# A two-layer kernel on one core: block inverses of a head gathered into one step of its loop, gram products one step further ahead

## The chip, the cores and the metric

The kernel runs on one NeuronCore of a Trainium2 chip. Its engines are TensorE (PE), VectorE (DVE), ScalarE (ACT), GpSimd (POOL) and SyncE (SP), which here only issues transfers. Each takes its instructions in the order in which they are written, and engines wait for one another by semaphores. The metric is the device time of one execution in microseconds, lower is better. The kernel before was timed three times: 1269.07, 1272.46 and 1273.2 us, median 1272.46 us.

## The reference

The input is `x` of 4 batches, 256 rows and 256 columns. Two layers follow one another, each an attention block and a feed-forward block behind a modulated layer norm. The change lies in the attention block of the first layer, a gated delta rule over 16 key heads with two value heads each:

```python
qkvz = hidden_states @ W_qkvz                 # per key head: q, k (128 each), v, z (256 each)
conv = silu(sum(xp[:, j:j + Tv, :] * conv_w[:, j] for j in range(4)))   # over q, k, v
beta = jax.nn.sigmoid(b)
alpha = jnp.exp(-jnp.exp(A_log) * jax.nn.softplus(a + dt_bias))
q = _l2norm(q) * DK ** (-0.5)
k = _l2norm(k)
def step(S, inp):                             # one row of the sequence after the other
    q_t, k_t, v_t, a_t, b_t = inp
    S = S * a_t[..., None, None]
    err = jnp.einsum('bhkv,bhk->bhv', S, k_t)
    v_new = (v_t - err) * b_t[..., None]
    S = S + k_t[..., None] * v_new[..., None, :]
    o = jnp.einsum('bhkv,bhk->bhv', S, q_t)
    return (S, o)
og = o * _silu(z)
og = og * jax.lax.rsqrt(jnp.mean(og * og, axis=-1, keepdims=True) + EPS) * norm_weight
return og.reshape(Bv, Tv, VDIM) @ W_out
```

The kernel computes the recurrence in blocks of 128 rows. For each value head and each half of the sequence, the rows of `v_new` are the solution of a triangular system of size 128.

## The kernel before, in words

The first layer runs as a loop of 64 steps: key head `kh` from 0 to 15 outside, batch `b` from 0 to 3 inside. A step of each engine is written in `pe_step`, `act_step`, `dve_step`, `pool_step`. In step (kh, b) several stages lie side by side, for different batches. `beside` picks the batch that is so many steps ahead.

- **q and k, 8 steps ahead** (`LEAD_QK`): `pe_qk` multiplies, `act_tap0` and `dve_tap` do the convolution in place, and `act_silu_qk` ends it.
- **Gram products, 7 steps ahead** (`LEAD_GRAM`): `pe_gram0` and `pe_gram1` form k·k and q·k. DVE scales them (`dve_scales`, `dve_scan`, `dve_bp`) into the block tiles `BP`, of which there are eight, two key heads by four batches.
- **v and z, 3 steps ahead** (`LEAD_VZ`), in the same manner, with a transpose of v (`pe_vt`) one step later.
- **The solve of this step**: `pe_solve` multiplies with the inverse of the triangular blocks in `UT` and with `BP`. `act_y` and `dve_r2` carry the pieces between its three parts. `pe_o` gives the output, `dve_og` gates it.
- **The output of the step before**: `act_ss` sums the squares (line 693), `pool_ro` takes the power -0.5 on GpSimd (line 998), `act_ogn` scales (line 701), `pe_ot` transposes (line 444), `act_ots` evicts (line 724), `pe_f` multiplies with the output weights (line 454), and `dve_acc` adds.

The inverses take a way of their own. The 32-row diagonal blocks of the next key head go from `BP` to a scratch tensor in HBM (`sp_blocks_in`, line 1076) and back into `Dm`, where each of 64 partitions holds one block (`sp_blocks_turn`, line 1085). GpSimd inverts all 64 at once by elimination (`pool_inverse`): for j from 0 to 30 one product (line 1023) and one subtraction (line 1026), each waiting for the one before. Those 31 pairs are dealt out over the four steps of a key head by `SPLIT`: 7, 12, 7 and 5 pairs, and `pool_ro` of the same step stands behind them in GpSimd's order. ACT writes the transpose `Tt` in two halves, in steps 2 and 3 (`act_turn`, line 718). Both results go out to HBM (`sp_blocks_out`, line 1097) and come back, spread over partitions, into `U` and `UT` (`sp_blocks_read`, lines 1107 and 1112). There `pe_merge` builds the inverses of size 64 and 128 out of those of size 32, in four phases. Each is a run of small matmuls into one PSUM bank (bank 7), with an eviction by ACT behind it (`act_merge`): the product of the diagonal (lines 391 and 392), the 32-row parts (394 to 396), the lower 64-row part (398), the upper one (400). Step 0 merges batches 0 and 1, step 1 merges batches 2 and 3. Steps 2 and 3 have no merges.

All transfers are issued by SP in one order that is written out by hand in its block: for each key head the turn, the reads, the loads of weights and of `alb`, the blocks of three batches, the out-transfer, the reads of the first two batches. A transfer whose condition isn't met holds up those written behind it.

## Time and profile before

| | |
|---|---|
| median of three timed runs | 1272.46 us |
| lowest, highest | 1269.07, 1273.2 us |
| span of the profiled execution | 1270.6 us |
| PE busy | 1168.6 us (92%) |
| VectorE busy | 914.6 us (72%) |
| ScalarE busy | 831.6 us (65%) |
| GpSimd busy | 751.5 us (59%) |
| GpSimd on the elimination, lines 1023 and 1026 | 551.8 us |

The page gives a span for the profiled execution, from its first to its last instruction, and no time beside it. The span lies within the three timed runs. The busy time of an engine is the time in which one of its instructions ran. For PE it hides that matmuls follow one another in a pipe. Busy time is an average over the whole program. The loop of the first layer takes up the stretch from about 105 to 1075 us, and only that stretch is touched.

### The profile page before, as it was taken

How to read it: one execution, taken by the hardware profiler on the slowest of the kernel's cores; microseconds unless marked ns; L12 is line 12 of the kernel's file. 1: busy time of each engine (PE TensorE's matmuls, PEld its weight loads, DVE VectorE, ACT ScalarE, POOL GpSimd, SP SyncE). 2: the span in 40 equal slices, each digit the busy share in tenths (PEclk: the TensorE clock that was granted, in tenths of full speed). 3: DMA queues.
4: the chain of work that ended last, by engine and by line, in shares of the span. 5: the costliest groups of instructions: out<-in, count | busy, mean ns of one | idle time of the engine just before them, and what ended most of it. 6: DMA issues, size and time to landing. Idle time of an engine off the chain costs nothing. (4 is left out here: it accounts for less than half of the span.)

```text
span 1270.6 us, 30469 instructions
## 1 busy us (share of the span) xinstructions
PE 1168.6 (92%) x10744; PEld 1002.5 (79%) x10744; DVE 914.6 (72%) x2304; ACT 831.6 (65%) x2289; POOL 751.5 (59%) x1187
## 2 busy tenths in 40 slices
PE   7787998999999999999999999999998688998986
PEld 6687887888888888888888888888887577776754
DVE  6786787788879797878888888879793414337764
ACT  6334776777777676777777777777675556218973
POOL 3275758586867777776858586858676601104211
PEclk9776999999999999999999999999998979999988
DMA  5212134314040313121222314040214130002000
GB/s 177 64 55 51 66 73 44 83 34 111 7 112 19 99 31 87 37 80 40 80 45 73 65 52 111 6 113 14 62 29 129 25 108 1 1 1 72 2 10 25
DMA packets 143430, 72.82 MB, mean 57 GB/s; under 512 B 116744, under 2 KB 132624, under 8 KB 141360
## 3 DMA queue, kind: packets, MB, share of 16 engines
q1 hardware_dynamic: 143280, 70.89, 22.5%
q8 instruction: 86, 1.41, 0.5%
q14 instruction: 64, 0.52, 0.1%
HBM read 57.06 MB, written 13.78 MB: 56 GB/s over the span
## 5 line engine op out<-in xcount | busy, mean ns | idle before, releaser
L1023 POOL TENSOR_TENSOR tmp<-Dm,Tn 64x31 f32<-64x31 f32 (+15 forms) x496 | 260.5, 525 | 104.0 <-DMA Dm<-blk_in_scratch 69.9
L1026 POOL TENSOR_TENSOR Tn<-Tn,tmp 64x31 f32<-64x31 f32 (+15 forms) x496 | 291.3, 587 | 38.8
L832 DVE SCALAR_TENSOR_TENSOR cv<-bank,cw,cv 128x255 f32<-128x255 f32 (+2 forms) x384 | 155.2, 473 | 145.0 <-ACT cv L631 144.8
L832 DVE SCALAR_TENSOR_TENSOR cqk<-bank,cw,cqk 128x255 f32<-128x255 f32 (+2 forms) x384 | 155.0, 472 | 16.5 <-ACT cqk L631 16.4
L998 POOL TENSOR_TENSOR ro<-ss,mhalf 128x4 f32<-128x4 f32 x64 | 68.0, 1062 | 158.2 <-issue 97.7
L892 DVE SCALAR_TENSOR_TENSOR BP<-bank,cj,E 128x512 f32<-128x512 f32 (+1 forms) x256 | 140.4, 611 | 2.6 <-DVE cj L877 0.3
L454 PE MATMUL bank<-wo,OTs 128*128 128x256 f32 x512 | 132.1, 392 | 0.9 <-ACT OTs L724 0.9
L693 ACT ACTIVATE junk<-og 128x129 f32<-128x129 f32 x256 | 79.6, 311 | 51.6 <-issue 39.4
L701 ACT ACTIVATE ogn<-og,ro 128x128 f32<-128x128 f32 x256 | 81.9, 393 | 44.4 <-POOL ro L998 44.1
L433 PE MATMUL bank<-Y,BP 128*128 128x128 f32 x512 | 95.7, 290 | 7.4 <-ACT Y L664 6.1
L454 PEld LDWEIGHTS bank<-wo,OTs 128*128 128x128 f32 x512 | 91.3, 193 | 12.0 <-ACT OTs L724 1.0
L338 PE MATMUL bank<-hh,wvz_hi 128*128 128x256 f32 x256 | 84.2, 329 | 9.0 <-ACT hT L645 9.0
L433 PEld LDWEIGHTS bank<-Y,BP 128*128 128x128 f32 x512 | 73.0, 193 | 19.4 <-ACT Y L664 19.4
L348 PE MATMUL bank<-wvz_hi,hh 128*128 128x256 f32 x256 | 83.7, 327 | 0.9
L308 PE MATMUL bank<-hh,wqk_hi 128*128 128x256 f32 x256 | 80.4, 314 | 3.1 <-DVE cqk L832 3.1
L664 ACT ACTIVATE Y<-bank 128x256 f32<-128x256 f32 x128 | 48.9, 382 | 51.6 <-PE bank L420 50.5
L318 PE MATMUL bank<-sqk 128*128 128x512 f32 x128 | 67.9, 613 | 8.8 <-DVE BP L892 8.8
L308 PE MATMUL bank<-hh,wqk_lo 128*128 128x256 f32 x256 | 74.8, 292 | 0.0
L308 PE MATMUL bank<-hl,wqk_hi 128*128 128x256 f32 x256 | 74.6, 292 | 0.0
L338 PE MATMUL bank<-hh,wvz_lo 128*128 128x256 f32 x256 | 74.2, 290 | 0.0
L338 PE MATMUL bank<-hl,wvz_hi 128*128 128x256 f32 x256 | 74.0, 289 | 0.0
L348 PE MATMUL bank<-wvz_hi,hl 128*128 128x256 f32 x256 | 73.2, 286 | 0.0
(210 smaller groups left out, 3326.9 us busy)
## 6 DMA issues: line engine op xcount, KB each, us to landing
rvz<-in_L_attn_W_qkvz SPq DMA_DIRECT2D x16, 512.0 KB, 5.5
x<-alpha_scratch SPq DMA_DIRECT2D x8, 1024.0 KB, 6.6
alb<-alpha_scratch SPq DMA_DIRECT2D x7, 1024.0 KB, 6.3
rqk<-in_L_attn_W_qkvz SPq DMA_DIRECT2D x16, 256.0 KB, 2.6
wo<-in_L_attn_W_out SPq DMA_DIRECT2D x16, 256.0 KB, 6.2
blk_in_scratch<-BP SPq DMA_DIRECT2D x256, 16.0 KB, 1.5
tinv_scratch<-Tn SPq DMA_DIRECT2D x32, 128.0 KB, 2.2
tinv_t_scratch<-Tt SPq DMA_DIRECT2D x32, 128.0 KB, 2.2
```

What stands on the lines that cost most here:

```text
L308: last = nc.tensor.matmul(bQK[:, t * T:(t + 1) * T], wqk[p][w][:, k, t * DK:(t + 1) * DK], h[:, k, b * T:(b + 1) * T], start=(k + n == 0), ...
L338: last = nc.tensor.matmul(bV[:, t * T:(t + 1) * T], wvz[p][w][:, k, t * DK:(t + 1) * DK], h[:, k, b * T:(b + 1) * T], start=(k + n == 0), ...
L348: last = nc.tensor.matmul(bZ[:, c * 256:(c + 1) * 256], h[:, k, b * T + c * P:b * T + (c + 1) * P], wvz[p][w][:, k, R * DK:2 * R * DK], st ...
L433: last = nc.tensor.matmul(o, block_of(p, b, h, 0, 0, c), Y[:, 0, h, :], start=True, stop=(c == 0))
L454: last = nc.tensor.matmul(bF[:, c * D:(c + 1) * D], OTs[:, h, c, :], wo[p][:, h, :], start=(h == 0), stop=(h == R - 1))
L693: nc.scalar.activation(junk[:], og[b % 2][:, c, h, :], ACT.Square, accum_out=ss[b % 2][:, n:n + 1]).then_inc(sem("ss"), 1)
L701: nc.scalar.activation(ogn[:, c, h, :], og[b % 2][:, c, h, 0:DK], ACT.Copy, scale=ro[b % 2][:, n:n + 1]).then_inc(sem("ogn"), 1)
L832: nc.vector.scalar_tensor_tensor(d, bk[:, t * T:(t + 1) * T - s], cw[p][:, first + t, TAPS - 1 - s:TAPS - s], d, ALU.mult, ALU.add).then_i ...
L892: nc.vector.scalar_tensor_tensor(dst, g, cj[i][:, c, h:h + 1], e, ALU.mult, ALU.mult).then_inc(sem("bp"), 1)
L998: nc.gpsimd.tensor_tensor(ro[b % 2][:], ss[b % 2][:], mhalf[:, 0:4], ALU.pow).then_inc(sem("ro"), 1)
L1023: pool_step_done(nc.gpsimd.tensor_tensor(t, Dm[:, j, j + 1:BLK].unsqueeze(2).broadcast_to([SLOTS, r, c]), Tn[:, j, 0:c].unsqueeze(1).broad ...
L1026: pool_step_done(nc.gpsimd.tensor_tensor(Tn[:, j + 1:BLK, 0:c], Tn[:, j + 1:BLK, 0:c], t, ALU.subtract), kh * NTS + 2 * j + 4)
```

## The change

The gram products, and with them the block tiles, move one step further ahead, from 7 to 8 steps, and q and k from 8 to 9. The block tiles become a ring of nine (`bp_of`) instead of two sets of four. All four batches of a key head merge in step 0 (`merges`), so that steps 1 to 3 have no merges. The phases now take all batches at once for the 32-row parts. The 64-row parts run as lower of batches 0 and 1, then lower of 2 and 3 alternating with upper of 0 and 1, then upper of 2 and 3. GpSimd's elimination is dealt out over steps 0 to 2, as 16, 5 and 10 pairs, and the blank start of the next one moves from step 0 to step 3. The four blocks' return into `Dm` is now a single transfer of 256 KB behind the reads, where it was two groups of four. The reads of `U` and `UT` take all four batches at once, in 3 and 4 transfers of twice the size. Both weight splits move to step 0. Some small tiles share memory with others to make room.

The core of the diff:

```diff
             E2 = sb("E2", [P, R, P], ctx=s1)
 
-            BP = [BP0, sb("BP1", [P, B, 6 * R, P], ctx=s1)]
-            Dm = sb("Dm", [SLOTS, BLK, BLK], ctx=s1)
+            BP1 = sb("BP1", [P, RING - B, 6 * R, P], ctx=s1)
+
+            def bp_of(kh, b):
+
+                n = (kh * B + b + RING - 1) % RING
+                return BP0[:, n] if n < B else BP1[:, n - B]
+
...
-            LEAD_QK, LEAD_GRAM, LEAD_VZ = 2 * B, 2 * B - 1, 3
+            LEAD_QK, LEAD_GRAM, LEAD_VZ = 2 * B + 1, 2 * B, 3
...
+            def pe_merge_64(kh, low, high):
+
+                wait(nc.tensor, "u_evac", kh * U_EV + (3 if high is None else 5 if high == 0 else 7))
+                lows = slots(range(2 * low, 2 * low + 2)) if low is not None else ()
+                highs = slots(range(2 * high, 2 * high + 2)) if high is not None else ()
+                for n in range(2 * NC * R):
+                    if lows:
+                        last = merge_low(kh, *lows[n])
+                    if highs:
+                        last = merge_high(kh, *highs[n])
                 last.then_inc(sem("u_mm"), 1)
...
             def merges(b):
-                return b < 2
+                return b == 0
...
                     if last:
                         pe_ot(*last, 2 * (now + 2))
-                    pe_merge(kh, p, b, 1)
                     if vz:
                         pe_v(*vz, 1, (1,))
+                    pe_merge_32(kh)
                     if last:
                         pe_f(*last, 0)
-                    pe_merge(kh, p, b, 2)
-                    if last:
                         pe_f(*last, 1)
-                    pe_merge(kh, p, b, 3)
+                    pe_merge_64(kh, 0, None)
                     if vz:
                         pe_z(*vz, 0)
-                    pe_solve(kh, p, b, 0)
+                    pe_merge_64(kh, 1, 0)
                     if vz:
                         pe_z(*vz, 1)
+                    pe_solve(kh, p, b, 0)
+                    pe_merge_64(kh, None, 1)
                     pe_solve(kh, p, b, 1)
                     if vt:
...
                 if merges(b):
                     if last:
                         act_ogn(*last)
-                    act_merge(kh, p, b, 0)
+                    act_merge_diag(kh)
                     act_before_ots(kh, b)
                     if last:
                         act_ots(*last)
-                    act_merge(kh, p, b, 1)
                     if vz:
                         act_tap0(*vz, "v", bV, cv, 2)
+                    act_merge_32(kh)
                     if qk:
                         act_tap0(*qk, "qk", bQK, cqk, 0)
-                    act_merge(kh, p, b, 2)
-                    act_merge(kh, p, b, 3)
+                    act_merge_low(kh, 0)
                     if vz:
                         act_silu_v(*vz)
+                    act_merge_high(kh, 0)
+                    act_merge_low(kh, 1)
                     act_y(kh, p, b, 0)
-                    splits(kh, p, b, act_split_qk, act_split_vz)
                     if qk:
                         act_silu_qk(*qk)
+                    act_merge_high(kh, 1)
                     if vz:
                         act_silu_z(*vz)
                     act_y(kh, p, b, 1)
                     if vt:
                         act_vs(*vt)
+                    splits(kh, p, b, act_split_qk, act_split_vz)
                 else:
                     act_y(kh, p, b, 0)
...
+                if kh and exists(kh + 1, 0, 0):
+                    split_vz(kh + 1, 1 - p)
+                if exists(kh + 3, 0, 0):
                     split_qk(kh + 3, 1 - p)
-                if b == 0 and kh and exists(kh + 1, 0, 0):
-                    split_vz(kh + 1, 1 - p)
...
                     dve_acc(*last)
                 if merges(b):
-                    dve_r2(kh, p, b)
-                    splits(kh, p, b, dve_split_qk, dve_split_vz)
                     ahead = beside(kh, p, b, LEAD_GRAM + 1)
                     if ahead:
                         scans(ahead, 0, R)
-                    dve_og(kh, p, b)
+                    dve_r2(kh, p, b)
                     if ahead:
                         scans(ahead, R, 2 * R)
+                    dve_og(kh, p, b)
+                    splits(kh, p, b, dve_split_qk, dve_split_vz)
 
...
-            SPLIT = ((0, 7), (7, 19), (19, 26), (26, BLK - 1))
-            LAST_SPLIT = ((0, 6), (6, 14), (14, 21), (21, BLK - 1))
+            SPLIT = ((0, 16), (16, 21), (21, BLK - 1))
...
             def pool_step(kh, p, b):
-                if kh + 1 < NKH:
-                    if b == 0:
-                        pool_vpow(kh + 1, 1 - p)
-                        pool_inverse_start(kh + 1)
-                    pool_inverse(kh + 1, *(SPLIT if kh + 2 < NKH else LAST_SPLIT)[b])
+                if b < len(SPLIT) and kh + 1 < NKH:
+                    pool_inverse(kh + 1, *SPLIT[b])
+                if b == B - 1 and kh + 2 < NKH:
+                    pool_inverse_start(kh + 2)
                 pool_ro(kh, p, b)
+                if b == 0 and kh + 1 < NKH:
+                    pool_vpow(kh + 1, 1 - p)
 
...
-            def sp_blocks_turn(kh, lo, hi):
-                for b in range(lo, hi):
+                                      bp_of(kh, b)[r, 0:4 * R:2, r]).then_inc(sem(f"blk_dr{b}"), 16)
+
+            def sp_blocks_turn(kh):
+                for b in range(B):
                     wait(nc.sync, f"blk_dr{b}", (kh + 1) * 16 * NBLK)
                 wait(nc.sync, "t_step", kh * NTS)
-                for n in range(NBLK):
-                    s = slice((n * B + lo) * PER_B, (n * B + hi) * PER_B)
-                    nc.sync.dma_start(Dm[s].rearrange("s j i -> s (j i)"),
-                                      blkin_dr[n, lo:hi].rearrange("b c h j i -> (b c h) (j i)")).then_inc(sem("blk_in"), 16)
...
+            def sp_blocks_read(kh):
+                wait(nc.sync, "y", at(kh, 0, 2))
                 wait(nc.sync, "t_out0", (kh + 1) * 32)
                 for n in range(NBLK - 1):
...
                 wait(nc.sync, "t_out1", (kh + 1) * 32)
                 for n in range(NBLK):
...
-                    sp_blocks_in(kh + 1, B - 1)
-                    sp_blocks_turn(kh + 1, B - 1, B)
-                    sp_blocks_read(kh, 1)
+                    ahead = kh + 2 < NKH
+                    if ahead:
+                        sp_blocks_in(kh + 2, 0)
                     if kh + 3 < NKH:
-                        sp_load_qk(kh + 3)
                         sp_load_alb(kh + 3)
-                    if kh + 2 < NKH:
+                    if ahead:
                         sp_load_vz(kh + 2)
...
-                    if kh + 2 < NKH:
-                        for b in range(B - 1):
-                            sp_blocks_in(kh + 2, b)
+                    if ahead:
+                        sp_blocks_in(kh + 2, 1)
+                        sp_blocks_in(kh + 2, 2)
+                    if kh + 4 < NKH:
+                        sp_load_qk(kh + 4)
                     sp_blocks_out(kh + 1)
-                    sp_blocks_read(kh + 1, 0)
-                sp_blocks_read(NKH - 1, 1)
+                    if ahead:
+                        sp_blocks_in(kh + 2, B - 1)
+                    sp_blocks_read(kh + 1)
+                    if ahead:
```

The other hunks write the phases of `pe_merge` and `act_merge` as functions of their own (`pe_merge_diag`, `pe_merge_32`, `merge_low` and `merge_high` with the same matmuls; `act_merge_diag` and `act_merge_32` with evictions of twice the width; `act_merge_low` and `act_merge_high` with the same as before). They also double the tile `nrm`, move one qk product, one gram product and one weight split from the loop into the code ahead of it, and place small tiles.

GpSimd around the start of a key head, where `ro` is the power of a step's output, `vsc` that of the scales, and `tmp<-Dm,Tn` and `Tn<-Tn,tmp` are one pair of the elimination. Before:

```order
L1023 TENSOR_TENSOR tmp<-Dm,Tn 64x31
L1026 TENSOR_TENSOR Tn<-Tn,tmp 64x31
L998 TENSOR_TENSOR ro<-ss,mhalf 128x4
L993 TENSOR_TENSOR vsc<-nrm,npow 128x16
L1012 MEMSET Tn 64x1024
L1013 AFFINE_SELECT Tn<-Tn 64x1024
L1023 TENSOR_TENSOR tmp<-Dm,Tn 64x31
L1026 TENSOR_TENSOR Tn<-Tn,tmp 64x31
```

In the changed kernel, where `DT` holds `Dm` and `Tt`:

```order
L1048 TENSOR_TENSOR Tn<-Tn,tmp 64x31
L1021 TENSOR_TENSOR ro<-ss,mhalf 128x4
L1034 MEMSET Tn 64x1024
L1035 AFFINE_SELECT Tn<-Tn 64x1024
L1021 TENSOR_TENSOR ro<-ss,mhalf 128x4
L1045 TENSOR_TENSOR tmp<-DT,Tn 64x31
L1048 TENSOR_TENSOR Tn<-Tn,tmp 64x31
```

and behind the first 16 pairs of the same key head:

```order
L1045 TENSOR_TENSOR tmp<-DT,Tn 64x256
L1048 TENSOR_TENSOR Tn<-Tn,tmp 64x16x16
L1021 TENSOR_TENSOR ro<-ss,mhalf 128x4
L1016 TENSOR_TENSOR vsc<-nrm,npow 128x16
L1045 TENSOR_TENSOR tmp<-DT,Tn 64x255
L1048 TENSOR_TENSOR Tn<-Tn,tmp 64x15x17
```

The blank start now stands ahead of the last `ro` of the key head before. Between that `ro` and the next one stand 16 pairs, where there were 7 with `vsc` and the blank start ahead of them.

SP from the out-transfers of one key head to the blocks of the next. Before:

```order
L1097 DMA tinv_scratch<-Tn 32x1024 x2
L1097 DMA tinv_t_scratch<-Tt 32x1024 x2
L1107 DMA U<-tinv_scratch 32x8x32 x3
L1112 DMA UT<-tinv_t_scratch 32x8x32 x4
L1085 DMA Dm<-blk_in_scratch 12x1024 x4
L1076 DMA blk_in_scratch<-BP 32x4x32 x4
L1085 DMA Dm<-blk_in_scratch 4x1024 x4
L1107 DMA U<-tinv_scratch 32x8x32 x3
L1112 DMA UT<-tinv_t_scratch 32x8x32 x4
```

In the changed kernel:

```order
L1114 DMA tinv_scratch<-Tn 32x1024 x2
L1114 DMA tinv_t_scratch<-DT 32x1024 x2
L1097 DMA blk_in_scratch<-BP 32x4x32 x4
L1122 DMA U<-tinv_scratch 32x16x32 x3
L1127 DMA UT<-tinv_t_scratch 32x16x32 x4
L1104 DMA DT<-blk_in_scratch 64x1024
L1097 DMA blk_in_scratch<-BP 32x4x32 x4
L1075 DMA x<-alpha_scratch 128x2048
```

The return into `Dm` stood ahead of the second reads, in two parts with the blocks of the fourth batch between them. Now it is one transfer, and all reads stand ahead of it.

PE at the 64-row parts of step 0. `U,BP` is the lower part, `UT,A2` the upper one. Before:

```order
L338 MATMUL bank3<-hl,wvz_hi1 128x256
L454 MATMUL bank5<-wo0,OTs 128x256 x2
L398 MATMUL bank7<-U,BP1 64x64 x8
L454 MATMUL bank5<-wo0,OTs 128x256 x2
L400 MATMUL bank7<-UT,A2 64x64 x8
L348 MATMUL bank3<-wvz_hi1,hh 128x256
```

In the changed kernel:

```order
L476 MATMUL bank5<-wo0,OTs 128x256 x4
L407 MATMUL bank7<-U,BP0 64x64 x8
L354 MATMUL bank3<-wvz_hi1,hh 128x256
L354 MATMUL bank3<-wvz_lo1,hh 128x256
L354 MATMUL bank3<-wvz_hi1,hl 128x256
L354 MATMUL bank3<-wvz_hi1,hh 128x256
L354 MATMUL bank3<-wvz_lo1,hh 128x256
L354 MATMUL bank3<-wvz_hi1,hl 128x256
L407 MATMUL bank7<-U,BP1 64x64
L411 MATMUL bank7<-UT,A2 64x64
L407 MATMUL bank7<-U,BP1 64x64
L411 MATMUL bank7<-UT,A2 64x64
```

The lower part of the second two batches now alternates, matmul by matmul, with the upper part of the first two. The output product `wo0,OTs` stands ahead of the first lower part as a whole.

## Rows read from the trace of the kernel before

**Rows 1.** Loop: stretch, us, busy PE, PEld, DVE, ACT, POOL (count), clock, DMA share, GB/s.
```profile
140.00:1050.00 910.00, 864.99 (x8550) 755.53 (x8550) 700.70 (x1588) 644.94 (x1721) 639.33 (x1008) 0.98 0.26 62
```

**Rows 2.** PE's timeline, first matmul of a step: start us, us, engine line operation.
```profile
235.91 0.59 PE L318 MATMUL bank<-sqk 128*128 128x512 f32 x1
...
593.38 1.02 PE L318 MATMUL bank<-sqk 128*128 128x512 f32 x2
...
610.59 0.59 PE L318 MATMUL bank<-sqk 128*128 128x512 f32 x1
...
627.43 0.59 PE L318 MATMUL bank<-sqk 128*128 128x512 f32 x1
...
640.13 0.59 PE L318 MATMUL bank<-sqk 128*128 128x512 f32 x1
...
652.51 0.59 PE L318 MATMUL bank<-sqk 128*128 128x512 f32 x1
...
950.56 0.59 PE L318 MATMUL bank<-sqk 128*128 128x512 f32 x1
```

**Rows 3.** PE's timeline in step 0 of a key head, phases of the merge.
```profile
597.81 0.21 PE L391 MATMUL bank<-U,BP 32*32 32x32 f32 x1
597.82 0.21 PE L392 MATMUL bank<-U,BP 32*32 32x32 f32 x1
...
598.31 0.19 PE L392 MATMUL bank<-U,BP 32*32 32x32 f32 x1
...
601.47 1.14 PE L398 MATMUL bank<-U,BP 64*64 64x64 f32 x16
```

**Rows 4.** GpSimd's timeline, same key head; brackets: idle time before, what ended it.
```profile
595.90 2.89 POOL L993 TENSOR_TENSOR vsc<-nrm,npow 128x16 f32<-128x16 f32 x1 [0.43 <-DVE nrm L872]
...
604.35 0.23 POOL L1023 TENSOR_TENSOR tmp<-Dm,Tn 64x31 f32<-64x31 f32 x1 [3.25 <-DMA Dm<-blk_in_scratch]
...
608.02 1.97 POOL L1026 TENSOR_TENSOR Tn<-Tn,tmp 64x135 f32<-64x135 f32 x1
...
613.26 1.05 POOL L998 TENSOR_TENSOR ro<-ss,mhalf 128x4 f32<-128x4 f32 x1 [0.75 <-POOL Tn L1026]
...
627.42 0.89 POOL L1023 TENSOR_TENSOR tmp<-Dm,Tn 64x255 f32<-64x255 f32 x1
```

**Rows 5.** VectorE's timeline, the two weight splits of that key head.
```profile
607.92 1.22 DVE L855 TENSOR_TENSOR wvz_lo<-rvz,wvz_hi 128x1024 fp32r<-128x1024 f32 x1
...
625.12 0.68 DVE L851 TENSOR_TENSOR wqk_lo<-rqk,wqk_hi 128x512 fp32r<-128x512 f32 x1
```

**Rows 6.** ScalarE and PE in step 2: scaled output and its transpose.
```profile
633.06 1.28 ACT L701 ACTIVATE ogn<-og,ro 128x128 f32<-128x128 f32 x4
...
634.39 0.33 PE L444 MATMUL bank<-eye,ogn 128*128 128x128 f32 x1 [0.42 <-ACT ogn L701]
```

**Rows 7.** Step 3: ScalarE's turn, SP's issues, and from the page a landing time.
```profile
648.44 1.11 ACT L718 ACTIVATE Tt<-Tn 64x512 f32<-64x512 f32 x1
...
645.22 1.73 SPq L1076 DMA_DIRECT2D blk_in_scratch<-BP  x4
...
649.57 0.78 SPq L1097 DMA_DIRECT2D tinv_t_scratch<-Tt  x2
650.88 1.33 SPq L1107 DMA_DIRECT2D U<-tinv_scratch  x3
652.26 1.93 SPq L1112 DMA_DIRECT2D UT<-tinv_t_scratch  x4
...
rqk<-in_L_attn_W_qkvz SPq DMA_DIRECT2D x16, 256.0 KB, 2.6
```

**Rows 8.** PE's idle spells in two steps, and a row of the busy table.
```profile
206.62 0.71 PE L420 MATMUL bank<-R,UT 128*128 128x128 f32 x4 [2.77 <-issue]
...
971.25 1.11 PE L444 MATMUL bank<-eye,ogn 128*128 128x128 f32 x4 [2.95 <-ACT ogn L701]
...
973.00:975.00 2.00, 2.00 (x27) 1.76 (x22) 0.00 (x0) 1.59 (x6) 1.76 (x4) 0.50 0.92 334
```

More of the change, by code:

```diff
@@ L798, in act_step @@
                         act_vs(*vt)
-                    if b == B - 1:
+                    if not merges(last[2]):
                         act_ogn(*last)
@@ L802, in act_step @@
                         act_tap0(*qk, "qk", bQK, cqk, 0)
-                    if b < B - 1:
+                    if merges(last[2]):
                         act_ogn(*last)
@@ L809, in act_step @@
                     act_ots(*last)
[L810 removed]
+                    if kh + 1 < NKH and b >= 2:
                         act_turn(kh + 1, b - 2)
```

204 lines of the change are left out of this document (99 added, 105 removed).

## The prediction

> **What bounds the kernel now.** The busy times come first: over the loop PE is busy 865 of 910 us, and no other engine above 701 [rows 1]. Next comes PE's own timeline, to get the length of each step. One key head takes 17.2, 16.8, 12.7 and 12.4 us for its four steps, 59.1 us from 593.38 to 652.51 [rows 2]. The twelve key heads from 235.91 to 950.56 average 59.55 us [rows 2]. The first two steps are longer because they hold the merges. PE's idle time is 45 of 910 us, 2.9 per key head [rows 1]. One piece of it is a wait for the scaled output ahead of its transpose, 0.42 us here [rows 6]. So PE sets the pace, and the reader should see that the other engines wait for it.
>
> GpSimd comes closest to it, not by busy share but as a chain. It waits 3.25 us for `Dm`, starts its pairs at 604.35, 11.0 us into the key head [rows 4], and has to end them before ScalarE turns the second half at 648.44, 8.3 us into step 3 [rows 7]. Between them it has to give `ro`, without which the output of a step isn't scaled. That chain is what the change rearranges.
>
> **What the change does on PE.** No matmul goes away. Per key head two gathered steps become one. The first phase of a merge takes 0.53 us for two batches (597.81 to the last start 598.31 and its spacing), and so does the second roughly. A 64-row part takes 1.07 us for two batches, 16 passes from 601.47 with the next product behind them [rows 3]. Step 0 now has these once more: 0.53 + 0.53 for the 32-row phases and, if lower and upper parts run at the same time, one more 1.07. With 0.2 for one more change of shape, the new step 0 is 17.2 + 2.3 = 19.5 us. Step 1 becomes like step 2. PE alone would need 19.5 + 12.7 + 12.4 + 12.4 = 57.0 us, 2.1 less than the 59.1.
>
> Would the alternating halves overlap? Lines 391 and 392, which read different rows of the array and write different partitions of one bank, start 0.01 us apart, a pair every 0.03 us [rows 3]. I take full overlap. Without it the step costs 1.07 more. The Trainium skill, "TensorEngine Tiling (Array Packing)", Restrictions and Gotchas, says that different row tiles cannot access the same PSUM bank at once. By that rule the halves in bank 7 would run one after the other. The trace speaks against it for the 32-row pairs.
>
> The wider evictions, 256 to 512 columns, cost ScalarE no more in all, since there are half as many. They lie under v, the transposes and both output products. Weight splits at the end of step 0 and the earlier scans hide in VectorE's idle time, which grows in step 0. The gram product one step earlier costs nothing in the loop.
>
> **What it does to GpSimd's chain.** Two things move. The reads are now all issued ahead of the return into `Dm`, and 16 pairs stand ahead of the first `ro`. I follow them from step 3, times counted from that step's start (640.13 in the trace):
> - the turn of the second half ends at 9.4, and `Tt` goes out from 9.4 to 10.2 [rows 7];
> - blocks of the fourth batch 1.7, reads of `U` 1.3, reads of `UT` 1.9 [rows 7], with gaps of 0.1 each: the return is issued at 15.6. The reads are twice as large, but SP's issue time goes by count, and the count is the same;
> - a transfer of 256 KB lands 2.6 us after issue [rows 7]: `Dm` is there at 18.2, which is 5.8 us into the next step 0. That is 5.2 earlier than now.
>
> From there (counted from step 0), 16 pairs. In the trace they take from 604.35 to 627.42 less 1.8 for the `ro` between them, 21.3 us [rows 4]. That figure contains the slowing by both weight splits: the subtraction at 608.02 took 1.97 us under the split at 607.92 [rows 4, 5]. In the new order both splits again fall into the 16 pairs, so I keep 21.3. It could be 2 less if they missed each other, and hardly more. The Trainium skill, "SBUF — State Buffer", Who interferes with whom, says a VectorE instruction with two SBUF inputs blocks one of GpSimd that reads SBUF. The trace agrees.
>
> So the pairs end at 27.1, `ro` takes 1.05 [rows 4] to 28.2, and the scaling 1.28 [rows 6] to 29.5. The transposes start at 29.6. Without waiting they would stand at 19.5 + 6.5 = 26.0, since in step 2 they stand 6.96 after the step's start with 0.42 idle [rows 2, 6]. **PE waits 3.6 us** in step 1 of each key head. Queued behind the transposes on PE are the third solve, the output, its product and z, and on ScalarE behind the scaling the first tap of v. From transposes to the end of the step are 5.7 us [rows 2, 6], so step 2 starts at 35.3. The other two steps end at 60.3 us.
>
> The remaining pairs fit this length. After `ro` come the scale power, 2.89 [rows 4], 5 pairs (6.7 at the mean of the sixteen, 21.3 / 16) and `ro`, ending 28.2 + 10.7 = 38.9, 3.6 into step 2. Then come 10 pairs, at most 13.3 at that mean and less since their sizes fall, and `ro`, ending at most 5.6 into step 3. The scaling asks for them about 4 into each step (it ran at 633.06, 5.6 into step 2, behind a tap that now follows it [rows 6]). I add nothing, and keep 0.5 each for the range.
>
> **The clock.** After idle spells of 2.77 and 2.95 us PE ran slow: at 971.25 four transposes took 1.11 us, and the table has a granted clock of 0.50 at 973 [rows 8]. That is 1.2 instead of 2.4 GHz. A wait of 3.6 us in every key head should bring it down most times. The two microseconds of that row, with PE busy throughout, lose 1 us of work, and the slow stretch began before them and at 971.25 at the latest, so the spell there cost 2 or more. I take 2 per key head, between 1 and 3. So a key head takes 62.3 us, 2.75 above 59.55.
>
> **The sum.** Key heads 1 to 13 give 13 × 2.75 = +36. Key head 0 gets the same wait early, about +4. Key head 1 has a stall of 2.77 with its slow clock behind it [rows 8] that the new wait may cover, −3. In key head 14 PE waits for `ogn` already [rows 8] and the elimination bounds; it starts 5.2 earlier now. Key head 15 saves the 2.1 of the merges. Together I estimate −7. That makes +30. The profiled span is 1270.6 and the median 1272.5, so the forecast is about 1302; I say 1300 us.
>
> **The rivals.**
> - **A, GpSimd late but the clock stays.** A key head takes 60.3, 0.75 more: 13 × 0.75 − 6 = +4, 1277 us (1268 to 1284). For it: waits like the 0.42 us of rows 6 occur in every key head with the mean clock at 0.98 [rows 1]. Against it: both spells near 3 us brought it down.
> - **B, GpSimd in time, so PE bounds: faster.** A key head takes about 57.3: 13 × −2.25 and −8 at the ends, −37, 1235 us (1228 to 1246). It decides where the first `ro` is done by 24.6 us after the start of step 0, 3.6 us sooner than I have it. The whole chain, 31 pairs and three powers, would have to shrink too. For it: `Dm` lands after one transfer, and its landing and the pairs' slowing are the two terms I estimate. Against it: both together give perhaps 2.5.
> - **C, in between.** Pairs and landing 1.5 to 2.5 us faster, PE waiting 1 to 2 us with the clock up: a key head of 58.5, 13 × −1.05 − 6 = −20, 1252 us (1246 to 1267).
> - **D, the change's alternation doesn't do what it says.** The halves don't overlap, step 0 is 20.6, the wait in step 1 shrinks by the same 1.1 and the key head stays at 60.3. It then favours A's number, since the wait falls to 2.5. The rule of the Trainium skill on banks, quoted above, would make this the case.
>
> **How the numbers follow.** The forecast gets 0.46, A with D 0.23, C 0.17, B 0.14. The forecast's own range is 1284 to 1316 from the clock's 1 to 3 us and half a microsecond either way in `Dm`. The range 1246 to 1316 leaves out most of B and a little above. A measurement of this kernel tells about 0.3%, 3.8 us, from no change. Faster than 1268.7: B, C and a little of A, 0.32. Within: the middle of A, 0.12. Slower: 0.56.
>
> **What would show it.** Right: PE's `ot` transposes of step 1 wait for `ogn`, and that for `ro`, which follows GpSimd's sixteenth pair without a gap; idle 3 to 4 us before them once per key head; `Dm` landing 5 to 6.5 us into step 0; granted clock of 0.5 in short stretches over the whole loop; step 0 of 19 to 20 us, steps 2 and 3 at 12.4 to 13. Wrong: GpSimd waits for the sums of squares ahead of the first `ro`, or step 1 is under 14 us, or the clock stays at 1.0. If step 0 is over 21, an eviction or the read of `UT` is late, which I held for covered (the read lands about 5 us into the step, and the second phase stands at 7).

## The result, and the profile after

The changed kernel takes 1311.6 us (median, 1305.4 to 1315.3) and the kernel before 1270.8 beside it on the same chip: 1.031 times as long, 95% interval 1.027 to 1.035. Forecast were 1300 us, in a range of 1246 to 1316, and a slower kernel. The profiled execution has a span of 1313.6 us, 43.0 over the 1270.6 of before. Ratios and intervals here and below leave out three executions that lay far above the rest: one of 1326 us of the kernel before, one of 2700 and one of 4572 us of two later kernels.

The first look goes to the busy table, cut at PE's step starts. One key head of the changed kernel, and then a stretch of its second step and the whole loop (stretch, its length, busy time of PE, PEld, DVE, ACT, POOL, granted clock, DMA share, GB/s):

```profile
565.55:584.47 18.92, 18.82 (x315) 16.56 (x313) 12.82 (x29) 13.29 (x31) 10.92 (x22) 1.00 0.40 101
584.47:604.33 19.86, 14.79 (x91) 13.64 (x89) 13.18 (x29) 10.95 (x34) 18.25 (x23) 0.83 0.17 44
604.33:616.70 12.37, 12.28 (x90) 11.00 (x89) 11.26 (x28) 9.26 (x23) 10.40 (x22) 1.00 0.13 29
616.70:629.08 12.38, 12.29 (x90) 11.01 (x89) 11.06 (x29) 9.87 (x27) 3.43 (x3) 1.00 0.21 47
...
595.00:602.00 7.00, 5.93 (x24) 5.65 (x25) 3.30 (x8) 5.13 (x15) 6.53 (x8) 0.51 0.00 0
...
140.00:1080.00 940.00, 845.70 (x8470) 758.25 (x8468) 690.35 (x1576) 634.08 (x1647) 640.10 (x1020) 0.95 0.25 57
```

Before, the loop had PE busy 865 of 910 us at a clock of 0.98 [rows 1]. Now it is busy 846 of 940 at 0.95. In this key head steps 0, 2 and 3 have PE busy without a gap. All the idle time is in step 1, which holds no merge: 14.8 of 19.9 us busy, and the clock at half speed for part of it. Over eleven key heads the four steps average 19.4, 19.2, 12.4 and 12.4 us, 63.3 in all. Before they were 17.2, 17.1, 12.9 and 12.4, 59.55 [rows 2]. Step 0 is 18.9 us where nothing disturbs it. Its average is higher because three of the eleven waited 0.2 to 1.4 us ahead of 32-row products, for which the trace names no cause, and because the clock fell behind the longest of these waits: that step 0 took 22.0 us.

PE's timeline at the first merge phase shows where the 43 us are (start, duration, then the operation, idle time before it in brackets). The third row is the stall of one step 1:

```profile
123.98 0.18 PE L390 MATMUL bank<-U,BP 32*32 32x32 f32 x1 [1.64 <-DMA U<-tinv_scratch]
...
254.84 0.21 PE L390 MATMUL bank<-U,BP 32*32 32x32 f32 x1
...
596.07 1.11 PE L466 MATMUL bank<-eye,ogn 128*128 128x128 f32 x4 [5.07 <-ACT ogn L722]
...
1011.86 0.23 PE L390 MATMUL bank<-U,BP 32*32 32x32 f32 x1 [1.76 <-issue]
...
1069.52 0.18 PE L390 MATMUL bank<-U,BP 32*32 32x32 f32 x1 [0.16 <-issue]
```

The L390 rows are key heads 0, 2, 14 and 15. The same phases of the kernel before started at 113.79, 240.34, 953.55 and 1014.90. So the way to the first merge grew by 10.2 us (I put this down to the longer lead; no run tries it alone), key heads 0 and 1 by 4.3, the twelve key heads 2 to 13 by 43.8 (3.65 each). Key head 14 shrank by 3.7, and what comes after key head 15's merge by 11.6. The sum is +43.0.

GpSimd, ScalarE and SyncE at the same place tell what PE waited for. GpSimd's timeline:

```profile
566.41 1.01 POOL L1021 TENSOR_TENSOR ro<-ss,mhalf 128x4 f32<-128x4 f32 x1 [1.23 <-issue]
572.96 0.23 POOL L1045 TENSOR_TENSOR tmp<-DT,Tn 64x31 f32<-64x31 f32 x1 [5.54 <-DMA DT<-blk_in_scratch]
...
593.70 1.01 POOL L1021 TENSOR_TENSOR ro<-ss,mhalf 128x4 f32<-128x4 f32 x1
...
616.05 0.24 POOL L1048 TENSOR_TENSOR Tn<-Tn,tmp 64x31 f32<-64x31 f32 x1
...
626.66 0.94 POOL L1034 MEMSET Tn<- 64x1024 f32 x1 [7.86 <-ACT DT L739]
```

ScalarE's timeline, the scaling in step 1 and the turn in step 3:

```profile
594.74 1.28 ACT L722 ACTIVATE ogn<-og,ro 128x128 f32<-128x128 f32 x4 [4.74 <-POOL ro L1021]
...
561.61 1.10 ACT L739 ACTIVATE DT<-Tn 64x512 f32<-64x512 f32 x1
```

SyncE's issues in step 3 and the step after it, and from the page the landing time of the return, in us:

```profile
562.74 1.01 SPq L1114 DMA_DIRECT2D tinv_t_scratch<-DT  x2
563.84 1.81 SPq L1097 DMA_DIRECT2D blk_in_scratch<-BP  x4
565.75 1.44 SPq L1122 DMA_DIRECT2D U<-tinv_scratch  x3
567.23 2.08 SPq L1127 DMA_DIRECT2D UT<-tinv_t_scratch  x4
569.48 0.45 SPq L1104 DMA_DIRECT2D DT<-blk_in_scratch  x1
...
DT<-blk_in_scratch SPq DMA_DIRECT2D x16, 256.0 KB, 3.5
```

Read them as a chain. The turn ends 9.6 us into step 3, the return is issued at 16.3, and `Dm` is there at 572.96, 7.4 into step 0. Sixteen pairs take 20.7 us with nothing between them, `ro` follows without a gap, then the scaling, then PE after 5.07 us of idle time. The last pair ends at 616.29, 0.4 before step 3. ScalarE turns this result only in the middle of step 3: the turn starts at 625.15, 8.9 us behind the last pair. GpSimd has one more `ro` to do in that time and then stands idle for 7.9 us, until the turn is over. That delay is the key to the experiments.

### The profile page after: what moved, and what is told of

It is laid out like the page before. It is cut to its first block and busy times, and to the rows that moved or that the text cites. A ratio compares the mean times of both kernels' runs of the same rounds, so it can differ in the third digit from the quotient of the medians.

```text
span 1313.6 us, 30101 instructions
## 1 busy us (share of the span) xinstructions
PE 1157.3 (88%) x10744; PEld 1011.2 (77%) x10744; DVE 911.0 (69%) x2304; ACT 827.4 (63%) x2225; POOL 742.6 (57%) x1187
## 5 line engine op out<-in xcount | busy, mean ns | idle before, releaser
L1045 POOL TENSOR_TENSOR tmp<-DT,Tn 64x31 f32<-64x31 f32 (+15 forms) x496 | 256.1, 516 | 134.7 <-DMA DT<-blk_in_scratch 99.4
L1048 POOL TENSOR_TENSOR Tn<-Tn,tmp 64x31 f32<-64x31 f32 (+15 forms) x496 | 286.0, 577 | 38.9
L466 PE MATMUL bank<-eye,ogn 128*128 128x128 f32 x256 | 46.2, 310 | 78.7 <-ACT ogn L722 78.5
L476 PEld LDWEIGHTS bank<-wo,OTs 128*128 128x128 f32 x512 | 98.1, 202 | 14.2 <-issue 1.8
L455 PE MATMUL bank<-Y,BP 128*128 128x128 f32 x512 | 102.8, 315 | 1.5 <-ACT Y L686 0.2
L466 PEld LDWEIGHTS bank<-eye,ogn 128*128 128x128 f32 x256 | 32.9, 157 | 83.0 <-ACT ogn L722 82.8
L455 PEld LDWEIGHTS bank<-Y,BP 128*128 128x128 f32 x512 | 83.2, 220 | 10.9 <-ACT Y L686 10.9
L927 DVE SCALAR_TENSOR_TENSOR og<-bank,vsc,hT 128x256 f32<-128x256 f32 x128 | 55.9, 479 | 49.3 <-PE bank L457 49.3
L344 PE MATMUL bank<-hh,wvz_hi 128*128 128x256 f32 x256 | 80.7, 315 | 4.1 <-ACT hT L667 4.1
L1034 POOL MEMSET Tn<- 64x1024 f32 x16 | 15.1, 944 | 114.7 <-ACT DT L739 114.7
```

The costliest lines, as they stand in the source:

```text
L344: last = nc.tensor.matmul(bV[:, t * T:(t + 1) * T], wvz[p][w][:, k, t * DK:(t + 1) * DK], h[:, k, b * T:(b + 1) * T], start=(k + n == 0), ...
L455: last = nc.tensor.matmul(o, block_of(kh, b, h, 0, 0, c), Y[:, 0, h, :], start=True, stop=(c == 0))
L466: last = nc.tensor.transpose(bOT[:, n * P:(n + 1) * P], ogn[:, c, h, :], ident)
L476: last = nc.tensor.matmul(bF[:, c * D:(c + 1) * D], OTs[:, h, c, :], wo[p][:, h, :], start=(h == 0), stop=(h == R - 1))
L1045: pool_step_done(nc.gpsimd.tensor_tensor(t, Dm[:, j, j + 1:BLK].unsqueeze(2).broadcast_to([SLOTS, r, c]), Tn[:, j, 0:c].unsqueeze(1).broad ...
L1048: pool_step_done(nc.gpsimd.tensor_tensor(Tn[:, j + 1:BLK, 0:c], Tn[:, j + 1:BLK, 0:c], t, ALU.subtract), kh * NTS + 2 * j + 4)
```

## The experiments

Theory: PE's wait in step 1 is one chain through GpSimd, and only the chain's placement is at fault. Rival: the merged step itself is dearer on PE, and the wait for `ro` is its shadow.

**The turn at the front of step 3** (in `act_step`).

```diff
                 else:
+                    if kh + 1 < NKH and b == B - 1:
+                        act_turn(kh + 1, 1)
                     act_y(kh, p, b, 0)
...
-                    if kh + 1 < NKH and b >= 2:
-                        act_turn(kh + 1, b - 2)
+                    if kh + 1 < NKH and b == 2:
+                        act_turn(kh + 1, 0)
```

> Edit: ScalarE turns the second half of the inverses at the front of step 3 instead of behind its output eviction; all else as in the changed kernel. Theory (one chain through GpSimd): in the changed kernel the turn stands 9.6 us into step 3, the return into Dm is issued at 16.3 and lands at 19.8, 7.4 into step 0; 16 pairs, ro and the scaling follow and PE waits 5.1 us. The elimination is over 0.4 us before step 3 starts, so the turn can be 8 us sooner. The reads then wait for the last Y of step 3 (7.8 into the step), so the return gains 4.7 us of the 8. PE's wait goes from 5.1 to about 0.4 us, the clock stays up, a key head goes from 62.4 to about 57: 1240 us (1228 to 1262). Rival 1 (the pace is set by PE's merged step and its clock, the wait for ro is a shadow of it): the wait moves to another semaphore and the time stays within 5 us of 1311. Rival 2 (the landing of Dm is slowed by the transfers queued ahead of it, not by its issue): Dm gains under 2 us, 1285 us.

Measured 1234.2 us (0.972 of before, 0.968 to 0.977), and in a second run 1236.3 (0.971, 0.968 to 0.974). One instruction a key head, moved, gives back 77 us. GpSimd's timeline, the busy table of steps 3, 0 and 1, and ScalarE's turn:

```profile
533.61 0.23 POOL L1047 TENSOR_TENSOR tmp<-DT,Tn 64x31 f32<-64x31 f32 x1 [1.67 <-DMA DT<-blk_in_scratch]
...
554.33 1.01 POOL L1023 TENSOR_TENSOR ro<-ss,mhalf 128x4 f32<-128x4 f32 x1
```

```profile
517.30:530.00 12.70, 12.27 (x90) 10.99 (x89) 11.25 (x29) 9.88 (x27) 5.10 (x8) 1.00 0.38 74
530.00:549.00 19.00, 18.90 (x315) 16.63 (x314) 13.31 (x29) 13.38 (x31) 14.37 (x28) 1.00 0.27 82
549.00:562.40 13.40, 12.17 (x90) 11.04 (x89) 12.72 (x28) 10.92 (x34) 12.54 (x14) 1.00 0.25 65
```

```profile
519.53 1.11 ACT L739 ACTIVATE DT<-Tn 64x512 f32<-64x512 f32 x1 [0.98 <-POOL Tn L1050]
```

Both rivals are out: the time left 1311 far behind, and `Dm` gained 3.8 us. `Dm` now lands 3.6 us into step 0 (7.4 without the edit), the first `ro` starts at 24.3 (28.2), step 1 takes 13.1 us on average and the clock is 1.00. The shorter key head, 57.4 us, brings GpSimd near: its last pair ends 2.2 us into step 3, and ScalarE waits 0.98 for it.

**The return ahead of all reads** (as SyncE had it in part before).

```diff
-                    sp_blocks_read(kh + 1)
-                    if ahead:
-                        sp_blocks_turn(kh + 2)
+                        sp_blocks_turn(kh + 2)
+                    sp_blocks_read(kh + 1)
```

> Edit: SyncE issues the return into Dm ahead of the seven reads of U and UT, as in the kernel before; all else as in the changed kernel. Theory (one chain): the return is issued 3.6 us sooner (the issue time of the seven reads) and lands 3.6 to 4.5 sooner, since no reads are queued ahead of it (3.5 us from issue to landing now, 2.6 in the kernel before). PE's wait goes from 5.1 to 0.6 to 1.5 us and the clock mostly stays up: 1252 us (1240 to 1275). Reads of U and UT land 0.5 us later, which nothing waits for (the first merge phase stands 3.5 us into step 0 with its data there). Rival 1 (PE's merged step sets the pace): within 5 us of 1311. Rival 2 (reads become late when they move behind a 256 KB transfer): PE waits for U ahead of the first merge phase instead, over 1290 us.

Measured 1269.5 us (1.001, 0.998 to 1.005). The gain is there, but smaller, and a new wait with it. SyncE's issues, PE's timeline at the first merge phase of three key heads, and the busy table of the two steps 0 that hold the last two of them:

```profile
534.91 0.91 SPq L1097 DMA_DIRECT2D blk_in_scratch<-BP  x2
...
537.06 0.45 SPq L1104 DMA_DIRECT2D DT<-blk_in_scratch  x1
537.61 1.59 SPq L1122 DMA_DIRECT2D U<-tinv_scratch  x3
```

```profile
606.34 0.18 PE L390 MATMUL bank<-U,BP 32*32 32x32 f32 x1 [3.16 <-issue]
...
667.20 0.18 PE L390 MATMUL bank<-U,BP 32*32 32x32 f32 x1 [1.53 <-issue]
...
728.00 0.18 PE L390 MATMUL bank<-U,BP 32*32 32x32 f32 x1 [1.53 <-issue]
```

```profile
661.20:684.70 23.50, 21.87 (x314) 18.75 (x313) 12.77 (x29) 13.25 (x31) 17.56 (x32) 0.85 0.33 81
722.00:742.50 20.50, 18.86 (x315) 16.56 (x314) 13.35 (x29) 13.28 (x31) 14.27 (x28) 1.00 0.37 93
```

The return has to wait until the last blocks are in DRAM, 1.2 us behind their issue, and the reads of `U` stand behind that wait. In the changed kernel the reads cover it. Step 1 falls to 13.0 us on average, step 0 rises from 19.4 to 22.0. So the second rival is half right: `U` becomes late. Its reads are issued behind that wait, the first of them lands 3.1 us after issue where it took 2.0, and PE starts 0.1 us behind the landing of the third. PE's wait is only part of the price. In four of eleven key heads the granted clock was 0.50 for 7 to 10 us of step 0, behind waits of 1.4 to 3.2 us, and those steps took 3.1 to 4.6 us more than work and wait. The two waits of 1.53 us above differ in just this: step 0 took 23.5 us in one and 20.5 in the other. The landing of the return stayed at 3.5 us without any read ahead of it, so the reads ahead don't explain it. Here seven reads follow it at once, and no run has the return with nothing on either side.

**The first `ro` behind twelve pairs.**

```diff
-            SPLIT = ((0, 16), (16, 21), (21, BLK - 1))
+            SPLIT = ((0, 12), (12, 19), (19, BLK - 1))
```

> Edit: twelve pairs instead of sixteen ahead of the first ro, then 7 and 12 (16, 5, 10 before); all else as in the changed kernel. Neither Dm nor the end of the elimination moves, only ro. Theory (what hurts is that the first ro stands behind sixteen pairs): ro comes 4 x 1.4 = 5.6 us sooner, the wait of 5.1 us goes, the clock stays up: a key head of 56.5 to 57.5 us and 1240 us (1228 to 1262). It leaves GpSimd's chain as it is: 43.1 us from Dm's landing to the end, which then stands 50.5 into a key head whose step 3 needs it at 53.3. Rival (the whole chain over a key head bounds, and the wait for ro only shows where its slack went): the wait comes back as one for the turn or for Dm, and the time stays above 1290.

Measured 1279.5 us (1.008, 1.005 to 1.011), where 1240 was expected. The busy table of steps 1 to 3:

```profile
504.80:517.20 12.40, 12.16 (x90) 11.03 (x89) 12.14 (x28) 10.24 (x32) 10.17 (x12) 1.00 0.25 69
517.20:531.60 14.40, 12.51 (x90) 11.02 (x89) 12.29 (x28) 9.60 (x27) 12.84 (x22) 1.00 0.11 24
531.60:546.20 14.60, 12.53 (x90) 11.05 (x89) 11.78 (x29) 9.79 (x27) 7.55 (x14) 1.00 0.19 42
```

Step 1 has lost its wait, 19.2 to 12.5 us, and the clock holds. But steps 2 and 3 take 14.4 and 14.6, and in both ScalarE waits about 2 us for `ro` ahead of the scaling. Ahead of the second `ro` now stand the scale power and seven pairs of the largest size, about 2.9 + 7 x 1.4 + 1.0 = 13.7 us, more than a step of 12.4, and twelve ahead of the third. My expectation counted the first and the last due time and not the two between. So of the 6.7 us won in step 1, 4.3 came back. That `ro` is what PE waits for in step 1 is shown all the same.

**All three at once: early turn, return ahead of the reads, six pairs already in step 3.**

```diff
+            SPLIT = ((6, 15), (15, 20), (20, BLK - 1))
...
                     pool_inverse_start(kh + 2)
+                    pool_inverse(kh + 2, 0, 6)
                 pool_ro(kh, p, b)
```

> Edit: turn at the front of step 3, return ahead of the reads, and 6 of the 31 pairs already in step 3 (then 9, 5, 11). Theory: Dm lands about 2 us before step 0 starts, the pairs start at once, the first ro is there well before it is asked for, and PE alone sets the pace: 18.9 + 3 x 12.4 = 56.1 us a key head instead of 62.4, 13 of them and a few at the ends: 1230 us (1220 to 1240), and the granted clock at 0.98 or more over the loop. Rival 1 (a bound of another engine close behind): GpSimd's 31 pairs, four ro and one power need 44 us and the turn at the front of step 3 stands 43.7 into the key head, so that ScalarE may wait there: 1240 to 1255. Rival 2 (PE's merged step and its clock set the pace): over 1290.

Measured 1260.2 us (0.993, 0.990 to 0.996): 26 us worse than the early turn alone. GpSimd's timeline at the end of step 3, then PE's in step 0:

```profile
537.33 0.72 POOL L1047 TENSOR_TENSOR tmp<-DT,Tn 64x31 f32<-64x31 f32 x1 [5.36 <-DMA DT<-blk_in_scratch]
...
543.37 1.01 POOL L1023 TENSOR_TENSOR ro<-ss,mhalf 128x4 f32<-128x4 f32 x1
```

```profile
545.75 0.66 PE L466 MATMUL bank<-eye,ogn 128*128 128x128 f32 x4 [2.03 <-ACT ogn L722]
```

`Dm` landed only as step 0 began, and the fourth `ro` now stood behind the six pairs that wait for it. Moving work ahead of a due instruction gives it that work's wait as well. Its own first rival came true in part: ScalarE waits 1.5 us in this step 3 for the end of the elimination, and step 3 takes 13.3 us where the early turn alone had 12.75. Step 0 takes 20.7 instead of 18.95, steps 1 and 2 a little less. The rival that PE's merged step sets the pace (over 1290) is refuted here too. What each of the three edits contributes, this one run can't tell.

**A filler on PE during the wait** (`pe_fill`: 36 products of 256 columns into the free bank).

```diff
+                    if b == 1 and vz and kh:
+                        pe_fill(*vz, 2 * (now + 3))
                     pe_ot(*last, 2 * (now + 3))
```

> Edit: the changed kernel, with 36 extra products of 256 columns on PE in step 1, right ahead of the transposes that wait for the scaled output; they read v's operands, write the free bank and are read by nobody (36 x 0.12 = 4.3 us of the 5.1 that PE waits there). Theory (the idle spell brings the granted clock down to 0.5, and that costs 2.4 us of the 7.5 that step 1 takes over 12.4): the clock stays at 1.0, step 1 goes from 19.9 to 17.5 us, a key head from 63.3 to 60.9, and the kernel from 1311 to 1280 us (1270 to 1290) although PE does 4.3 us more a key head. Rival (the drop of the clock comes from something else than the idle spell, or costs nothing since PE waits anyway): 1305 to 1315 us. Rival 2 (ro isn't late by the time I read, and the products delay it): over 1315.

Measured 1293.5 us (1.020 of before, 1.015 to 1.025), 18 less than the changed kernel and 13 above the expectation. The busy table of a step 1 and of the loop:

```profile
389.40:406.80 17.40, 16.61 (x126) 15.48 (x126) 13.06 (x28) 10.87 (x34) 16.04 (x20) 1.00 0.19 51
...
140.00:1080.00 940.00, 896.99 (x9123) 807.28 (x9122) 705.88 (x1594) 650.09 (x1697) 640.66 (x1018) 0.99 0.26 60
```

More work on PE makes the kernel faster, since the clock stays at 1.00. Step 1 falls to 17.4 us, near the 17.5 expected. But I had started from one key head of 19.9 us, and the average is 19.2: in five of the eleven the fall of the clock had cost only 1.1 to 1.3 us instead of 2.4. Step 2 grows by 0.4. The kernel gets 1.5 us a key head out of it (63.3 to 61.8).

**Small pairs, in both kernels.** Every pair works on one element of a partition instead of up to 256. So both kernels leave out the elimination, while order and waits stay, and they price PE nearly alone.

```diff
-                    r, c = BLK - 1 - j, j + 1
+                    r, c = 1, 1
```

> Edit: the changed kernel with each of GpSimd's 31 pairs working on one element a partition instead of up to 256; the elimination itself is left out, order and semaphores stay. Theory (PE alone needs 18.9 + 3 x 12.4 = 56.1 us a key head; all the rest is GpSimd's chain and the clock): sixteen pairs take 10 us instead of 20.7, the first ro is in time, the granted clock stays at 1.0 in the loop, a key head takes 56.1 to 56.5, 13 x 7 = 91 us less, and the elimination ahead of the first key head and in the last but one shrink by about 15 each: 1190 us (1175 to 1205). Rival (the merged step itself is slow: its evictions, its banks or the reads of U and UT): a key head over 58 us, and waits in step 0.

> Edit: the kernel before with the same small pairs on GpSimd; the elimination is left out. Theory (PE sets the pace of the kernel before, at 59.1 us a key head, and the merge of two gathered steps into one saves PE 3.0 of them): a key head stays at 59.0 to 59.5, the ends shrink by about 35: 1233 us (1220 to 1245), 43 above the changed kernel with the same edit. Rival (the kernel before also waited for GpSimd, and the merge saves PE less than 1.5 us): within 20 us of the changed kernel with the same edit.

Measured 1211.9 us (0.953, 0.951 to 0.956) for the changed kernel and 1253.8 (0.988, 0.983 to 0.994) for the kernel before. PE's steps take 19.2, 12.5, 12.4, 12.4 = 56.5 us and 17.2, 16.9, 12.5, 12.4 = 58.9. The merge of two gathered steps saves PE 2.4 us a key head, 39 over sixteen, and the two kernels differ by 42 us where GpSimd is out of the way: 43 were expected. Both times came out over the expectation, by 22 and 21. The key heads came out as expected, so the miss lies in the ends, which I had taken to shrink by more. The kernel before gains 17 us here, and only 0.64 a key head in the loop: it was bound by PE.

**Lower and upper parts in a row**, on the kernel with the early turn.

```diff
-                for n in range(2 * NC * R):
-                    if lows:
-                        last = merge_low(kh, *lows[n])
-                    if highs:
-                        last = merge_high(kh, *highs[n])
+                for low in lows:
+                    last = merge_low(kh, *low)
+                for high in highs:
+                    last = merge_high(kh, *high)
```

> Edit: the kernel with the turn at the front of step 3 (a key head of 57.2 us, near PE's own 56.1), and in the phase that holds both parts of the 64-row merge the sixteen lower parts issued in a row and then the sixteen upper ones, instead of alternating. Theory (the two overlap: in the trace they start 0.006 us apart, a pair each 0.058 us): the phase takes 1.8 us instead of 0.93, a key head is 0.9 us longer: 1234 + 14 x 0.9 = 1247 us (1243 to 1251). Rival 1 (they don't overlap, the starts are only issue times): no difference, 1234. Rival 2 (slack in step 0 hides it): the phase is longer in the trace, the time is 1234.

Measured 1240.6 us (0.977, 0.974 to 0.981), 4 to 6 over the two runs of its base, where 13 were expected. PE's timeline in the changed kernel, where they alternate:

```profile
577.60 0.22 PE L407 MATMUL bank<-U,BP 64*64 64x64 f32 x1
577.60 0.22 PE L411 MATMUL bank<-UT,A 64*64 64x64 f32 x1
577.66 0.22 PE L407 MATMUL bank<-U,BP 64*64 64x64 f32 x1
577.66 0.22 PE L411 MATMUL bank<-UT,A 64*64 64x64 f32 x1
```

Two parts of a pair start within 0.01 us of each other, and pairs follow at 0.06. Step 0 grew from 18.95 to 19.7 us in a row, so the two do overlap, and that is worth 0.8. The key head grew by 0.3 only: the steps behind it had small waits that shrank in exchange, step 1 from 13.1 to 12.9. The intervals of the two kernels touch, so the time alone shows this only weakly; the step does.

**The return between the reads of `U` and of `UT`**, with the early turn and alone.

```diff
             def sp_blocks_read(kh, turn=None):
...
+                if turn is not None:
+                    sp_blocks_turn(turn)
                 wait(nc.sync, "t_out1", (kh + 1) * 32)
```

> Edit: the kernel with the turn at the front of step 3, and SyncE issues the return into Dm between the three reads of U and the four of UT. Theory (after the turn is early, what is left over PE's own 56.5 us a key head is still GpSimd's chain: Dm lands 3.6 us into step 0, the first ro ties with its transposes, and the elimination ends 2.2 us into step 3): the return goes 2.1 us sooner (the issue time of the reads of UT), U isn't moved, UT lands 0.5 later with 3 us to spare; a key head 57.4 to 56.8, 1226 us (1220 to 1232). Rival 1 (the return waits for the last blocks to land in DRAM, as in the kernel with the return ahead of all reads, so it gains under 1 us): 1232 to 1236. Rival 2 (UT becomes late): over 1240.

> Edit: the changed kernel with only the return moved between the reads of U and of UT; the turn stays where it was. Theory (ro's lateness is the wait): Dm lands 2.1 us sooner, PE's wait goes from 5.1 to 3.0 us with U in time; the clock falls as before in about half of the key heads: a key head 63.3 - 2.1 - 0.7 = 60.5, 1274 us (1266 to 1285). With the return ahead of all reads PE waited for U in one key head of three (25 us in step 0); here it shouldn't, so if that and not ro was the cost there, this one is at 1245 or below. Rival (the return waits for the blocks to land): 1295.

With the early turn 1225.8 us (0.964, 0.960 to 0.967), alone 1272.8 (1.001, 0.998 to 1.004); expected 1226 and 1274. The first is the fastest kernel of the study that does all the work. Its busy table, steps 0, 1 and 3:

```profile
471.00:489.90 18.90, 18.80 (x314) 16.54 (x313) 13.46 (x29) 13.27 (x31) 15.85 (x30) 1.00 0.23 69
489.90:502.60 12.70, 12.46 (x91) 11.06 (x90) 12.39 (x28) 10.20 (x31) 11.86 (x13) 1.00 0.25 67
...
515.00:527.70 12.70, 12.28 (x91) 11.00 (x90) 11.26 (x29) 9.88 (x27) 5.03 (x8) 1.00 0.36 69
```

A key head takes 56.75 us, within 0.3 of what PE needs with the small pairs. In the kernel with the return alone it takes 60.3: step 0 is back at 19.2, so `U` is in time, and step 1 takes 16.2. Its waits there are between 2.2 and 3.8 us. So the return ahead of all reads and the return between them cost about the same time by different waits. PE's timeline at two of them:

```profile
274.01 0.66 PE L466 MATMUL bank<-eye,ogn 128*128 128x128 f32 x4 [3.40 <-ACT ogn L722]
...
333.76 1.11 PE L466 MATMUL bank<-eye,ogn 128*128 128x128 f32 x4 [3.39 <-ACT ogn L722]
```

**The turn a little later**, behind the first `Y` and the scaling of V, in the fastest kernel.

> Edit: as the kernel with the early turn and the return between the reads, but the turn stands behind the first Y and the scaling of V in step 3, ahead of the scaling of the output, so that ScalarE doesn't hold the first Y back when the elimination ends after the step has started. Theory: ScalarE waited 1.0 us at the front of step 3 for the elimination, which PE felt by 0.3; within 3 us of the kernel with the turn at the very front, on either side. Rival (ScalarE's order at the front of step 3 is what keeps a key head at 57.4): 8 us or more faster.

Measured 1236.0 us (0.972, 0.969 to 0.975), 10 us slower than the turn at the very front, so both the theory and its rival missed. ScalarE's timeline in step 3 of this kernel, and then of the fastest one:

```profile
522.71 0.38 ACT L686 ACTIVATE Y<-bank 128x256 f32<-128x256 f32 x1 [1.61 <-PE bank L442]
523.15 0.84 ACT L678 ACTIVATE Vs<-bank,vsc 128x256 f32<-128x256 f32 x2
524.01 1.13 ACT L739 ACTIVATE DT<-Tn 64x512 f32<-64x512 f32 x1
```

```profile
517.16 1.11 ACT L739 ACTIVATE DT<-Tn 64x512 f32<-64x512 f32 x1 [0.97 <-POOL Tn L1050]
518.29 0.38 ACT L686 ACTIVATE Y<-bank 128x256 f32<-128x256 f32 x1
```

At the very front the turn lies in a gap in which ScalarE waits for PE anyway, 1.6 us here. Behind `Y` the whole 1.1 us pushes back the scaled output and the taps. PE then waits 0.9 us for `cv` ahead of z, where it waited 0.4: step 3 takes 13.7 us instead of 12.6. I looked at who waits for ScalarE's first instruction and not at what its last ones cost.

The kernel with the early turn was timed once more beside these, as the yardstick:

> The kernel with the turn at the front of step 3 once more, beside the two that build on it: 1234 us (1230 to 1237) as before, the yardstick for differences under one per cent.

Measured 1236.3 us, as given above.

## Why the prediction was right, step by step

The mechanism was the one forecast, in the loop: the first `ro` late, PE idle ahead of the `ot` transposes of step 1, the clock down with it. The early turn and the filler show both parts by taking them away. The sum was +30 and became +43 in the profiled spans (41 in the medians). Two of the signs I had set were missed in size: 3 to 4 us of idle time in step 1, found 5.0 on average, and `Dm` 5 to 6.5 us into step 0, found 7.4.

- **PE's own work.** Forecast 19.5 + 12.7 + 12.4 + 12.4 = 57.0 against 59.1. With small pairs it is 56.5 against 58.9. Right, and a little better: 18.9 us for an undisturbed step 0.
- **The halves overlap.** Right: both parts of a pair start together, and in a row they cost 0.8 us more (I had 1.07). By the rule that I had cited from the Trainium skill, "TensorEngine Tiling (Array Packing)", Restrictions and Gotchas, different row tiles of one bank would have excluded this. The trace decides against it for 64-row tiles too, here with the two tiles writing different partitions of the bank. Rival D falls.
- **`Dm`.** Forecast 5.8 us into step 0, found 7.4. This is the term that was mis-sized, in two parts. The return was issued 16.3 instead of 15.6 us into step 3 (reads 2.1 and gaps instead of 1.9), and it landed in 3.5 instead of 2.6. I had taken the 2.6 of `rqk`, of the same 256 KB [rows 7]. The size alone doesn't give the landing: `wo`, also of 256 KB, took 3.7 in the changed kernel and 6.2 in the one before.
- **The sixteen pairs.** Forecast 21.3, found 20.7. In this key head the wait came to 5.1 us instead of 3.6: 1.6 from `Dm` and 0.6 from the shorter step 0, less 0.6 from the pairs. On average it is 5.0.
- **The clock.** Forecast 2 us per key head, between 1 and 3. Step 1 takes 19.2 on average, less 5.0 of idle time and 12.3 of work: 1.9. The filler brought back 1.5. Right in size. What I hadn't thought of is step 0: there too the clock fell once, behind a wait of 1.35 us.
- **The key head.** 62.3 forecast, 63.1 to 63.3 found, 12 times: +44 where +33 was counted for these twelve.
- **The ends.** Forecast +4 for key head 0, -3 on top of its 2.75 for key head 1, -7 for 14 and 15. Found +4.3 for key heads 0 and 1 together, and -15.3 for the tail. What I had left out was the way to the first merge, +10.2. All ends together are -0.8 where I had -3, so the miss of 13 us is the loop's 11 and 2 more. That the ends come out so near is luck: +10.2 was missing and the tail gave 8 more than I had, and the two cancel.
- **Steps 2 and 3.** "I add nothing" was right: 12.4 each. The third kernel shows how close that was.
- **Rival B** (PE bounds, 1235 us) is the truth of the same kernel with its turn moved, 1234.2 us. I had given it 0.14 because landing and pairs together would give perhaps 2.5 of the 3.6 us. I sought the missing time in durations, and it lay in a place: 8.9 us in which GpSimd's finished result waited to be turned. My own numbers had the last pair end 4.6 us into step 3 at most and the turn run from 8.3 to 9.4, and I didn't ask what stood between the two.

## What to carry to other kernels

Where a change moves a loop's work from one engine to another's chain, write down the chain with due times at each consumer, all of them, and look for a finished result that waits for a slot on a third engine: here one instruction of 1.1 us, moved into a gap, turned 3.1% slower into 2.8% faster. An instruction costs least in a place where its engine waits anyway, and work put ahead of a due instruction brings its own waits along. When a merge pays on the bound engine (2.4 us of 59 here), measure it once with the other chain shortened, so that the gain and the new wait are seen apart.

## What the runs showed of the hardware

- Three transfers of 256 KB from DRAM landed in different times in the changed kernel: `DT` into 64 partitions in 3.5 us, `rqk` into 128 in 2.6, and `wo`, issued right behind a load of 512 KB, into 128 in 3.7. `DT` took 3.5 us with seven reads issued just ahead of it, and also with none ahead and seven just behind. What sets the time wasn't tried.
- Idle time of PE against the clock: in the changed kernel, with waits of 2.4 to 6.2 us, all eleven steps 1 took 1.1 to 2.5 us more than work and wait, and behind the stall of the rows above the granted clock was 0.51, that is 1.2 GHz. In the kernel with the return alone between the reads, with waits of 2.2 to 3.8 us, seven of eleven did, by 1.1 to 1.5. The two rows above, with 3.40 and 3.39 us, differ: the transposes took 0.66 in one and 1.11 in the other, and the step 15.7 and 17.0. So a wait near 3 us has no fixed price. Nor is a shorter one safe: with the return ahead of all reads, waits of 1.4 to 3.2 us ahead of the small products of step 0 were followed by 7 to 10 us at a granted clock of 0.50 in four key heads of eleven, at a price of 3.1 to 4.6 us, and two waits of 1.53 us differed by 3 us.
- Products that nobody reads, put into a wait, kept the clock at 1.00 and paid for themselves by 18 us.
